# Layer norm, lightning attention and a routed FFN: third output buffer, moved steps in last chunks and heads, rotations straight out of PSUM

## The reference

```python
xn = layernorm(x)
# attention: 16 heads of 32, in blocks, with a decay per head
q, k, v, u = split(xn @ W_qkvu.T)            # q and k through silu
o  = (q * q_decay) @ kv + ((q @ k.T) * diag_decay) @ v
kv = block_decay * kv + (k * k_decay).T @ v  # carried from block to block
attn = (u * rms_norm(o)) @ W_out.T
# ffn on the 256 of the 2048 rows with the highest router score
idx = sort(top_k(xn @ w_router, 256)); s = xn[idx]
h = rms_norm(s) * ln1_w
q, k, v = h @ wq + bq, h @ wk + bk, h @ wv + bv   # 16 heads, 8 of k and v, of 128
q, k = rope(q, idx), rope(k, idx)
x1 = s + softmax(causal(q @ k.T) / sqrt(128)) @ v @ wo
mlp = silu(rms(x1) @ w_gate) * (rms(x1) @ w_up) @ w_down
out[idx] += gate * (x1 + mlp) + (1 - gate) * s      # other rows: xn
```

## Time and profile before

| | us |
|---|---|
| median of 3 runs | 572.98 (571.99 to 573.39) |
| profiled execution | 572.29 |
| its span | 570.6 |
| mean granted clock of PE | 0.961 |
| PE busy | 514.4 (90%) |
| DVE busy | 328.6 (58%) |
| ACT busy | 262.3 (46%) |
| POOL busy | 247.3 (43%) |

### The profile page before, as it was taken

One profiled execution on the slowest core, in us unless ns is written; L12 is line 12 of the kernel. 1 busy time (PEld: TensorE's weight loads), 2 busy tenths in 40 slices (PEclk: granted clock), 3 DMA queues, 4 the chain that ended last, 5 costly groups with the idle time before them and its releaser, 6 DMA issues.

```text
span 570.6 us, 11414 instructions
## 1 busy us (share of the span) xinstructions
PE 514.4 (90%) x4523; PEld 472.3 (83%) x4523; DVE 328.6 (58%) x613; ACT 262.3 (46%) x472; POOL 247.3 (43%) x207
## 2 busy tenths in 40 slices
PE   2979999999999999999999479889989997399994
PEld 2969899998999989999898469778967876399983
DVE  5988655754387787644547855778764643012331
ACT  7822232222276668232433337656676744253340
POOL 2062454333231333343386847243433333068973
PEclk9979999999999999999999787999998998799998
DMA  8733133211311001022224315543348331424532
GB/s 258 278 96 119 47 112 112 93 57 38 112 40 36 24 20 39 20 66 69 109 93 148 116 56 174 192 166 130 118 160 277 100 138 40 147 76 152 176 115 37
DMA packets 32884, 62.11 MB, mean 109 GB/s; under 512 B 3440, under 2 KB 3456, under 8 KB 32704
## 3 DMA queue, kind: packets, MB, share of 16 engines
q1 hardware_dynamic: 32288, 60.08, 31.5%
q0 software_dynamic: 544, 1.31, 1.2%
HBM read 48.27 MB, written 13.12 MB: 108 GB/s over the span
## 4 chain that ended last, share of the span: by engine, by line
PE 58%; issue 17%; POOL 10%; DVE 8%; ACT 5%; DMA 1%; SPq 0%; DVEq 0%; POOLq 0%; ACTq 0%
PE bank L1264 19%; PE bank L1218 7%; PE bank L1219 7%; PE bank L1220 7%; PE bank L1255 6%; POOL wlo L1162 5%; PE bank L1286 3%; DVE rope L897 2%; PE bank L1332 2%; PE bank L1322 2%; PE bank L1294 2%; PE bank L1316 2%; PE bank L1234 1%; DMA UR<-uo_all 1%; DVE rope L895 1%
## 5 line engine op out<-in xcount | busy, mean ns | idle before, releaser
L1162 POOL TENSOR_TENSOR wlo<-raw,whi 128x512 fp32r<-128x512 f32 x96 | 129.9, 1386 | 122.4 <-ACT whi L521 122.4
L1218 PE MATMUL bank<-HTh,whi 128*128 128x256 f32 x224 | 66.3, 296 | 14.4 <-DVE XR L932 9.7
L1219 PE MATMUL bank<-HTl,whi 128*128 128x256 f32 x224 | 65.8, 294 | 0.0
L1220 PE MATMUL bank<-HTh,wlo 128*128 128x256 f32 x224 | 65.5, 292 | 0.0
L1143 POOL TENSOR_TENSOR state<-kv_new,state_dec 128x512 f32<-128x512 f32 x15 | 21.8, 1454 | 94.7 <-DVE kv_new L834 94.7
L823 DVE TENSOR_TENSOR A<-bank,DEC 128x512 f32<-128x512 f32 x64 | 39.7, 683 | 37.2 <-PE bank L1286 35.7
L1218 PEld LDWEIGHTS bank<-HTh,whi 128*128 128x128 f32 x224 | 45.5, 203 | 15.4 <-issue 15.1
L521 ACT ACTIVATE whi<-raw 128x2048 fp32r<-128x2048 f32 x24 | 45.8, 1910 | 16.5 <-DMA raw<-in_w_down 12.5
L1219 PEld LDWEIGHTS bank<-HTl,whi 128*128 128x128 f32 x224 | 45.5, 203 | 0.2
L1220 PEld LDWEIGHTS bank<-HTh,wlo 128*128 128x128 f32 x224 | 45.4, 203 | 0.0
L1264 PE MATMUL bank<-xTh,WKh 128*128 128x256 f32 x128 | 38.6, 302 | 2.1 <-DVE WKl L764 2.1
(11 more groups left out here) (281 smaller groups left out, 1539.4 us busy)
## 6 DMA issues: line engine op xcount, KB each, us to landing
X<-in_x SPq DMA_DIRECT2D x16, 256.0 KB, 2.9
xn_all<-XN SPq DMA_DIRECT2D x16, 256.0 KB, 2.0
uo_all<-uo SPq DMA_DIRECT2D x16, 256.0 KB, 2.6
raw<-in_wq SPq DMA_DIRECT2D x4, 1024.0 KB, 5.3
UR<-uo_all SPq DMA_DIRECT2D x16, 256.0 KB, 5.6
XR<-in_x SPq DMA_DIRECT2D x16, 256.0 KB, 4.7
raw<-in_wo SPq DMA_DIRECT2D x4, 1024.0 KB, 5.6
out<-XR SPq DMA_DIRECT2D x16, 256.0 KB, 2.9
```

Of the source, the lines that this page charges most:

```text
L1162: ins = Q.tensor_tensor(low[:, k, :], raw[b % 2][:, k, :], high[:, k, :].bitcast(f32), ALU.subtract)
L1218: T.matmul(dst, lh, rh, start=first, stop=False)
L1219: T.matmul(dst, lh, rl, start=False, stop=False)
L1220: return T.matmul(dst, ll, rh, start=False, stop=last)
```

## The change

- XR has three buffers. `load_x_again(h + 2)` stands in head step h behind the load of uo and the store; the load of tile 15 so stands ahead of the late stores and of three block loads.
- `stage` reads the PSUM bank: for each of the two heads one operation of 128x256 and two of 64x256 (bias added, times cosine or sine), then the sum. `unit_bias` on ACT and qb are gone; the bank is free when the six operations are done.
- In slots 14 and 15, `gated` and `state_part` stand ahead of the rotation at position 2.
- In head step h, ACT's order is: unit_high, split_uo, exp, PTh, normalised(h), base, block_hi, OTh. normalised was of h-1 and stood first; block_hi stood last. DVE's reciprocal is of head h too.
- At the start, x's tiles 2 and 3 are loaded ahead of Q's and V's weights, four tiles (not three) belong to the first phase, K's weights are split in two halves around the first xT, U's low half is DVE's, BM and state are filled by POOL, the decay tables are made in three parts, and PE runs 12 and 6 products of the identity with itself (`awake`).

```diff
-NX, NXN = 3, 4
+NX, NXN, NXR = 3, 4, 3
...
-        qb = at("qb", 84, [P, 2, 2, SEL])
...
-        XR = at("XR", 140, [P, 2, DM])
+        XR = [at(f"XR{i}", kb, [P, DM]) for i, kb in enumerate((140, 142, 190))]
...
             def load_x_again(N):
                 if N < 2:
                     sp.wait_ge(tab_ps, 1)
+                elif N < NXR:
+                    for c in range(2):
+                        sp.wait_ge(uo_out[c], 16 * N_TILES // 2)
                 else:
-                    sp.wait_ge(stored[N % 2], 16 * (N // 2))
-                sp.dma_start(XR[:, N % 2, :], x_t[N]).then_inc(xr_in[N % 2], 16)
+                    sp.wait_ge(stored[N % NXR], 16 * (N // NXR))
+                sp.dma_start(XR[N % NXR][:], x_t[N]).then_inc(xr_in[N % NXR], 16)
...
             load_x(1)
-            for q, done, n in (("K", w_raw_k, 1), ("Q", w_raw_q, 0)):
-                for k in range(NK):
-                    sp.dma_start(raw_w[q][:, k, :], WT_v[:, k, n * DM:(n + 1) * DM]).then_inc(done[k], 16)
+            for k in range(NK):
+                sp.dma_start(raw_w["K"][:, k, :], WT_v[:, k, DM:2 * DM]).then_inc(w_raw_k[k], 16)
             load_x(2)
+            for k in range(NK):
+                sp.dma_start(raw_w["Q"][:, k, :], WT_v[:, k, 0:DM]).then_inc(w_raw_q[k], 16)
+            load_x(3)
             sp.dma_start(raw_w["V"][:], WT_v[:, :, 2 * DM:3 * DM]).then_inc(w_raw["V"], 16)
-            load_x(3)
             sp.dma_start(wr_b[:], w_router.partition_broadcast(P)).then_inc(wr_in, 16)
             sp.dma_start(raw_w["U"][:], WT_v[:, :, 3 * DM:4 * DM]).then_inc(w_raw["U"], 16)
             load_x(4)
-            for M in range(NX):
+            for M in range(NXN):
                 store_xn(M)
+            load_x(NXN + 1)
...
             load_block(6)
             for h in range(STEPS):
+                if h + 2 < N_TILES:
+                    load_uo(h + 2)
+                if h < late_outs[0]:
+                    store(h)
+                if h + 2 < N_TILES:
+                    load_x_again(h + 2)
                 if h in load_at:
                     load_block(block_of[load_at[h]])
-                if 2 <= h + 2 < N_TILES:
-                    load_uo(h + 2)
-                if 2 <= h + 1 < N_TILES - 1:
-                    load_x_again(h + 1)
-                if h < late_outs[0]:
-                    store(h)
             for b in range(block_of["U1"] + 1, len(order)):
                 load_block(b)
                 if b == block_of["U1"] + 1:
-                    store(late_outs[0])
-                    load_x_again(late_outs[2])
-                    store(late_outs[1])
-                    store(late_outs[2])
...
-            def unit_bias(u):
...
-                    ins = S.activation(qb[:, n % 2, i, :], job_bank("unit", u)[:, i * SEL:(i + 1) * SEL], ACT.Identity,
-                                       bias=bqkv[:, head:head + 1])
...
             decay_tables(0)
+            decay_tables(1)
+            first_weights_hi("K", w_raw_k, k_w_hi, (0, 1))
             xt_high(0)
             xt_high(1)
-            first_weights_hi("K", w_raw_k, k_w_hi)
-            first_weights_hi("Q", w_raw_q, q_w_hi)
-            decay_tables(1)
+            first_weights_hi("K", w_raw_k, k_w_hi, (2, 3))
+            first_weights_hi("Q", w_raw_q, q_w_hi, range(NK))
+            decay_tables(2)
...
                 p, g = h - PT_AT, h - PV_AT
-                if 0 <= h - 1 < FH:
-                    normalised(h - 1)
+                if h - 1 in unit_of_step:
+                    unit_high(unit_of_step[h - 1])
+                if h < late_outs[1]:
+                    split_uo(h + 1)
                 if h < FH:
                     act.wait_ge(sm_ok, h + 1)
                     if h >= 2:
...
-                if h - 1 in unit_of_step:
-                    unit_high(unit_of_step[h - 1])
-                if h < late_outs[1]:
-                    split_uo(h + 1)
                 if 0 <= p < FH:
...
-                if h in unit_of_step:
-                    unit_bias(unit_of_step[h])
+                if h < FH:
+                    normalised(h)
                 if h < late_outs[0]:
                     base(h)
+                if h in hi_after:
+                    block_hi(block_of[hi_after[h]])
                 if 0 <= g < FH:
...
-                if h in hi_after:
-                    block_hi(block_of[hi_after[h]])
...
-                dve.wait_ge(unit_b, n + 1), dve.wait_ge(cs_ok, 1)
+                dve.wait_ge(unit_ps, u + 1), dve.wait_ge(cs_ok, 1), dve.wait_ge(part_in, 16 * 5)
                 if n:
                     dve.wait_ge(staged_ok, n)
-                both = qb[:, n % 2]
                 half = P // 2
-                V.tensor_tensor(rope1[:], both, CS[:, 0, :].unsqueeze(1).to_broadcast([P, 2, SEL]), ALU.mult)
-                for a, b in ((0, half), (half, 0)):
-                    ins = V.tensor_tensor(rope2[a:a + half], both[b:b + half],
-                                          CS[b:b + half, 1, :].unsqueeze(1).to_broadcast([half, 2, SEL]), ALU.mult)
-                ch.link(ins)
+                for i in range(2):
+                    head = 4 * int(k[1]) + 2 * p + i + (FKV if k[0] == "Q" else 0)
+                    src, bias = job_bank("unit", u)[:, i * SEL:(i + 1) * SEL], bqkv[:, head:head + 1]
+                    V.scalar_tensor_tensor(out=rope1[:, i, :], in0=src, scalar=bias, in1=CS[:, 0, :], op0=ALU.add,
+                                           op1=ALU.mult)
+                    for a, b in ((0, half), (half, 0)):
+                        ins = V.scalar_tensor_tensor(out=rope2[a:a + half, i, :], in0=src[b:b + half],
+                                                     scalar=bias[b:b + half], in1=CS[b:b + half, 1, :], op0=ALU.add,
+                                                     op1=ALU.mult)
+                ins.then_inc(unit_b, 1)
+                dve.wait_ge(unit_b, n + 1)
                 V.tensor_tensor(staged[:, n % 2, :].rearrange("p (a m) -> p a m", a=2), rope1[:], rope2[:],
                                 ALU.add).then_inc(staged_ok, 1)
...
+            first_weights_lo("K", k_w_hi, k_w_lo, (0, 1))
             for M in range(CH):
                 xt_low(M)
-            first_weights_lo("K", k_w_hi, k_w_lo)
-            ln_stats(CH)
+            first_weights_lo("K", k_w_hi, k_w_lo, (2, 3))
+            for M in range(CH, NXN):
+                ln_stats(M)
             first_weights_lo("Q", q_w_hi, q_w_lo)
-            ln_norm(CH)
-            for M in range(NX):
+            for M in range(CH, NXN):
+                ln_norm(M)
+            first_weights_lo("V", v_w_hi, v_w_lo)
+            xt_low(CH)
+            first_weights_lo("U", u_w_hi, u_w_lo)
+            for M in range(NXN):
                 router(M)
-            first_weights_lo("V", v_w_hi, v_w_lo)
-            dve.wait_ge(decays_ok, 3), dve.wait_ge(masks_ok, 2)
+            dve.wait_ge(decays_ok, 4), dve.wait_ge(masks_ok, 2)
             V.tensor_tensor(DEC[:], DEC[:], tri[:].unsqueeze(1).to_broadcast([P, NH, P]), ALU.mult).then_inc(dec_ok, 1)
-            ch.link(V.memset(BM[:], 0.0))
-            for r in range(4):
-                V.memset(BM[DH * r:DH * r + DH, DH * r:DH * r + DH], 1.0)
-            V.memset(state[:], 0.0).then_inc(bm_ok, 1)
...
-                if N + XT_AHEAD < N_TILES:
+                if CH < N + XT_AHEAD < N_TILES:
                     xt_low(N + XT_AHEAD)
                 if N == CHOOSE:
                     place_tokens()
-                in_position(N, 2)
+                if N < N_TILES - CH:
+                    in_position(N, 2)
                 if N == HIDDEN:
                     hidden_low(0)
                     rotations()
...
                     gated(N)
                 if 0 <= N < N_TILES - 1:
                     state_part(N)
+                if N >= N_TILES - CH:
+                    in_position(N, 2)
                 if N == HIDDEN + 1:
                     selected_scores()
                 in_position(N, 3)
...
-                n, p, g = h - 1, h - PT_AT, h - PV_AT
-                if 0 <= n < FH:
-                    dve.wait_ge(exp_ok, n + 1)
-                    if n >= 2:
-                        dve.wait_ge(pn_ok, n - 1)
-                    V.reciprocal(pinv[:, n % 2, :], psum_[:, n % 2, :]).then_inc(sum_ok, 1)
+                p, g = h - PT_AT, h - PV_AT
                 if h < FH:
                     dve.wait_ge(sc_ps, h + 1)
                     if h >= 2:
...
                     unit_low(unit_of_step[h - 1])
                 if h < late_outs[1]:
                     uo_low(h + 1)
+                if h < FH:
+                    dve.wait_ge(exp_ok, h + 1)
+                    if h >= 2:
+                        dve.wait_ge(pn_ok, h - 1)
+                    V.reciprocal(pinv[:, h % 2, :], psum_[:, h % 2, :]).then_inc(sum_ok, 1)
                 if 0 <= p < FH:
...
-            ln_rstd(range(CH, NX))
+            Q.memset(state[:], 0.0)
```

(11 more changed lines are left out.)

81 lines of the change are left out of this document (37 added, 44 removed).

## The result

The changed kernel takes 554.72 us (median of 4, 553.98 to 555.70) against 573.18 before (4 runs beside it). The ratio is 0.966, with a 95% interval of 0.963 to 0.970: 18.5 us faster, where 26.2 were forecast. The profiled execution has a span of 552.5 us (570.6 before), so its own difference is 18.1.

A forecast was written before the change was run, and what follows sets the result against it. PE was taken as busy nearly throughout 40 to 310 us, so only holes outside and their slow clock could be won: 11.8 + 2.0 + 8.4 + 4.0 = 26.2, 572.98 - 26.2 = 546.8 us; range 538 to 557.

The forecast's parts named there:

- Tail, 11.8: Up product's 9.69 us hole goes through x15's earlier load: 9.7, plus 2.1 of slow clock; bounds 9.7 to 12.7.
- the chain that the prediction put at the low end: Tail: weight-block loads, two raw buffers waiting for POOL's low halves, could fix 39.3 us; then only 9.7 is won.
- Start, 2.0: Second group's first K product: xTl(3) ends 3.4 us earlier, less 1.4 for a slow restart; bounds 0 to 4.5.
- The slow restart: Start: PE pauses 2.5 to 2.8 us twice, so 1.4 us was taken off the gain.
- Price of a rotation, 3.7: Six operations out of PSUM at 0.48 each, plus 0.1 and the 0.69 sum: 3.7 us; per-operation bounds 0.40 and 0.85.
- Last chunks and first head steps, 8.4: PE's 14.7 us of holes from 313 to 390 shrink, leaving 3.7 and a new 2.6; bounds 5 to 13.
- the rotation's +0.9 on DVE and -0.8 on ACT cost nothing while both stay below 8.7: Head steps with a unit: PE bounds at 8.70 us, DVE 6.90 and ACT 7.40 busy, so the rotation's shift costs nothing.
- Later heads, 4.0: Heads after 419: normalised(h) within its step removes 5.1 us of PE holes and slow clock, less 1.1; bounds 2 to 5.
- a chain of DVE mask, ACT exp, DVE reciprocal, ACT PN is some 1.1 longer: Head steps 13 to 19: reciprocal and PN now fall within the step, a price of 1.1 us.
- R1: Rival: earlier stages win nothing, each term only shifts one wait to the next; 15.8 us won, 557.2; chance 0.14.

The follow-up runs named there:

- the run with the split rotation: Changed kernel with the rotation out of PSUM in the last two slots only; head-step units use ACT's bias into qb again; 547.76 us, ratio 0.958.

## Why the prediction was right and wrong

The sum was 26.2; 18.1 came in the profile. The time lies in the stated range, since the tail and most of the mechanisms came as said, but two of the four terms were much too large.

- **Tail, 11.8: measured 13.4.** The mechanism is right: the load of x's tile 15 is issued at 441.56 now, ahead of the blocks, and no wait is left before the up product. The 1.6 above it is a term I left out: behind the 2.28 us hole at G0, which both kernels have, the clock was 0.72 before and 1.00 after. That is luck, not the change: in the twelve programs that have all of the new tail and start, G0 to the end lies between 70.0 and 72.7, so the gain between 10.9 and 13.6. The buffers and the order of SP alone brought 8.4 in this stretch. What they leave is the chain that the prediction put at the low end: the last block's product starts 39.4 after D1's load is issued there (507.20 to 546.61), 39.3 before, and with the whole change 38.5 (501.41 to 539.90). Which part of the rest of the change takes away the wait of 2.91 is not shown.
- **Start, 2.0: measured 1.2.** The chain is right to within half a us: mask product done at 29.8 (30.05 said), K product at 43.1 (42.7 to 43.1 for xTl). Between them one step was off: x6's load was issued at 32.38, 1.4 later than said. The slow restart was sized 1.4 and cost 2.1 (clock 0.73 in the window above); the run with more dummy products shows the stretch without it.
- **Price of a rotation, 3.7: measured 3.7** (310.77 to 314.45), up to 0.9 more where its sum of two SBUF tensors meets POOL. 0.48 for each of the six, as taken, and the pair of 64 rows 0.98. The Trainium skill (VectorE: DVE Perf Modes, Two Vector instructions with no wait between them) gives just that, the full time for each half, and the trace agrees.
- **Last chunks and first head steps, 8.4: measured 3.8.** Up to out 0 it was 7.2, with POOL's second block done at 320.7 (321.5 said), and the holes 2.63 and 3.43 (3.7 and 2.6 said). The reason given for the smaller hole was wrong: kv_new's new place gives next to nothing beside the short rotation (2.63 against 2.93), which does it. What failed in size is the step "the rotation's +0.9 on DVE and -0.8 on ACT cost nothing while both stay below 8.7". In the row with 6.90 POOL ran 5.04 us, but mostly beside reads of PSUM and while DVE stood; in the changed kernel's step from 381 to 390 two low halves and a sum, 0.7 each alone, take 1.4 to 1.8 beside POOL, and DVE is busy 8.93 of 9.00. Moreover the bank is now free only at the end of DVE's step, not after ACT's copy. I had named both conditions (DVE over 8.7; DVE as PE's releaser in several steps) and given the outcome no price. By the run with the split rotation it is 4.7 up to out 5: 3.0 of idle time, the rest slow clock.
- **Later heads, 4.0: measured -0.1.** Won 5.2 from out 5 to out 12, as said (5.1), but PN's place is hardly the reason: with the old order 4.5 of it stays, and 1.6 come with the three buffers alone. So the number is right by luck. What failed is the size of "a chain of DVE mask, ACT exp, DVE reciprocal, ACT PN is some 1.1 longer": 5.3. I priced the chain of the new order and not what was put ahead of it on ACT: a conversion of 1.9 ahead of OTh (1.3 to 2.2 of idle time by the run without it). The idle time grew by 2.4 in all, and the slow clock that it brought (0.50 in the window behind 441.48) adds 2.9, a term that the prediction put at nothing here. The old order gives all back, 5.6.
- Of the rivals none came in whole; R1 (557.2) is nearest in size, but for another reason, since the chunks did win 7.2.

## What to carry to other kernels

Freeing a PSUM bank early can be worth a copy: an operation that reads PSUM directly saves the copy, but holds the bank until its place in a full engine's queue comes, so decide this by place in the program, as the split version does. Size an engine's room in a step with each of its two-SBUF-input operations at the price beside POOL, since another schedule will put POOL's work beside them. Where several parts are changed together, cut the profile at products that exist in both programs: the net here hid 10.8 us of losses, and undoing their causes brought some 7 back. Read each stretch's idle time and clock beside its length: several of the differences here were mostly clock.

## What the runs showed of the hardware that was not expected

- The same hole does not always cost the clock. Behind the 2.28 us hole at G0 matmuls go on starting every 0.12 us in six of the fourteen profiles here; in the other eight, the kernel before among these, they fall to one every 0.21 for a while. In the changed kernel the clock fell behind a hole of 1.74 (before 354.35); in the run with the slots' old order it did not fall behind the same hole of 1.74 (before 354.42). A hole's slow restart is to be priced as likely, not as certain.
- Contention between DVE and POOL is paid by both: POOL's four pieces take 6.36 beside a rotation from SBUF and 5.02 beside one from PSUM. The Trainium skill (SBUF - State Buffer, Who interferes with whom) calls the shared pair of ports an exclusive lock; the trace agrees in that each engine is slower beside the other.
- An operation with a single SBUF tensor as input (and one scalar a row) can be hit as well. XN (L719) takes 1.48 us beside POOL's low half of k and 0.54 without it, in the rows below. In both kernels each XN that runs beside a POOL operation of 128x512 takes 1.47 to 1.52 us, and each of the others 0.54 or 0.55. So it is not only operations with two SBUF inputs that have to be priced at the contended value:

```profile
38.22 1.48 DVE L719 TENSOR_SCALAR XN<-X,small 128x512 f32<-128x512 f32 x1 [0.60 <-POOL small L1100]
...
41.07 0.54 DVE L719 TENSOR_SCALAR XN<-X,small 128x512 f32<-128x512 f32 x1
...
38.15 1.25 POOL L1136 TENSOR_TENSOR kl<-KT,kh 128x512 fp32r<-128x512 f32 x1
```
